# Gathered rows split on chip into three bfloat16 parts before the sums of a two-layer graph network

## The reference

```python
def sage_conv(x, src, dst, W_l, b_l, W_r, n_nodes):
    agg = segment_sum(x[src], dst)            # sum of the gathered rows of each destination
    cnt = segment_sum(ones, dst)
    return agg / maximum(cnt, 1) @ W_l.T + b_l + x @ W_r.T

h = relu(sage_conv(x, ...)); x = layernorm(x + sage_conv(h, ...))
Q, K, V = x @ Wq.T + bq, x @ Wk.T + bk, x @ Wv.T + bv;  E = edge_attr @ We.T + be
score = exp(clip((K[src] * Q[dst] / 4 * E).sum(-1), -5, 5))       # per head of 16 features
x = layernorm(x + segment_sum(V[src] * score, dst))
```

## Time and profile before

| what | us |
|---|---|
| median of three runs (13885.14 to 13908.0) | 13896.76 |
| the profiled execution, its own time | 13876.17 |
| its span, from the first to the last instruction | 13874.4 |
| POOL busy in the span | 7767.2 (56%) |
| PE busy, and its weight loads | 7655.9 (55%), 6718.6 |
| DVE busy, ACT busy | 4877.0 (35%), 2823.4 (20%) |

### The profile page before, as it was taken

How to read it: one execution, slowest core, us unless ns; L and a number is a source line. 1 busy time by engine, 2 the same in 40 slices (tenths; PEclk the granted TensorE clock), 3 DMA queues, 4 the chain that set the end, 5 groups by cost and what they waited for, 6 DMA issues and landing times.

```text
span 13874.4 us, 192542 instructions
## 1 busy us (share of the span) xinstructions
PE 7655.9 (55%) x51633; PEld 6718.6 (48%) x51634; DVE 4877.0 (35%) x11774; ACT 2823.4 (20%) x4770; POOL 7767.2 (56%) x8221
## 2 busy tenths in 40 slices
PE   5556656566666555566655555444444544444554
PEld 4555545555555445455544545444444444444444
DVE  3333333333333323233333334333333333433334
ACT  1111111111111000000000003333333333333333
POOL 5555655555555555555555555555555555555554
PEclk7666666766666666666666666555555555555555
DMA  3222222222222112111111112333333333333333
GB/s 62 50 55 52 53 50 50 49 50 49 49 49 49 42 41 46 41 42 43 41 40 41 40 40 82 101 97 98 101 95 98 98 99 90 101 92 93 99 93 82
DMA packets 951617, 917.13 MB, mean 66 GB/s; under 512 B 484896, under 2 KB 740544, under 8 KB 950544
## 3 DMA queue, kind: packets, MB, share of 16 engines
q0 software_dynamic: 260000, 369.16, 12.8%
q1 hardware_dynamic: 605345, 430.43, 11.6%
q10 hardware_dynamic: 85325, 105.63, 2.2%
HBM read 789.35 MB, written 115.24 MB: 65 GB/s over the span
## 4 chain that ended last, share of the span: by engine, by line
PE 30%; issue 30%; another core or an unknown queue 23%; DVE 7%; DVEq 7%; ACT 2%; ACTq 0%; DMA 0%; POOL 0%; POOLq 0%; SPq 0%
PE ps_kv L763 4%; PE ps_kv L754 3%; PE ps_e L740 3%; PE ps_sum L723 2%; PE ps_q L723 2%; PE ps_kv L923 2%; PE ps_hot L723 2%; PE ps_t L732 1%; ACT node_q L1037 1%; PE ps_kv L772 1%; PE ps_sum L923 1%; PE ps_hot L923 1%; PE ps_kv L903 1%; PE ps_q L923 1%
## 5 line engine op out<-in xcount | busy, mean ns | idle before, releaser
L627 POOL DMA_INDIRECT kv<-kv_rows,src_ids x3125 | 2955.6, 946 | 2344.0 <-DVE message L1520 1412.2
L627 POOL DMA_INDIRECT kv<-in_x,src_ids x2500 | 2365.3, 946 | 1845.4 <-issue 912.1
L627 POOL DMA_INDIRECT kv<-h_rows,src_ids x2500 | 2367.1, 947 | 1801.5 <-issue 955.6
L754 PE MATMUL ps_kv<-between,hot 128*128 128x490 bf16 x2500 | 897.8, 505 | 976.2 <-ACT node_q L1037 553.9
L723 PE MATMUL ps_sum<-kv,hot 128*128 128x65 f32 x5000 | 937.9, 355 | 247.7 <-issue 210.5
L723 PEld LDWEIGHTS ps_sum<-kv,hot 128*128 128x128 f32 x5000 | 922.8, 277 | 270.9 <-issue 270.2
L1086 ACT ACTIVATE node_h<-node_h,unit 128x640 bf16<-128x640 f32 x722 | 1042.6, 1444 | 36.9 <-issue 8.1
L723 PE MATMUL ps_hot<-kv 128*128 128x65 f32 x1880 | 418.9, 400 | 1075.4 <-issue 885.8
L723 PEld LDWEIGHTS ps_hot<-kv 128*128 128x128 f32 x1880 | 391.7, 309 | 1148.8 <-issue 1146.7
L754 PEld LDWEIGHTS ps_kv<-between,hot 128*128 128x128 bf16 x2500 | 291.4, 130 | 1305.9 <-issue 995.8
L1306 DVE TENSOR_SCALAR between<-ps_t,message 128x980 bf16<-128x980 f16 x1250 | 898.7, 719 | 0.0
(11 more groups left out here) (253 smaller groups left out, 12432.2 us busy)
## 6 DMA issues: line engine op xcount, KB each, us to landing
node_h<-in_dst SPq DMA_DIRECT2D x625, 320.0 KB
node_q<-in_edge_attr SPq DMA_DIRECT2D x125, 480.0 KB
edge_space<-ee_rows SPq DMA_DIRECT2D x125, 480.0 KB
kv<-kv_rows,src_ids POOLq DMA_INDIRECT x3125
kv<-in_x,src_ids POOLq DMA_INDIRECT x2500
node_q<-in_edge_attr SPq DMA_DIRECT2D x125, 320.0 KB
kv<-h_rows,src_ids POOLq DMA_INDIRECT x2500
edge_space<-ee_rows SPq DMA_DIRECT2D x125, 320.0 KB
```

The source lines that it names most:

```text
L627: nc.gpsimd.indirect_dma_start(out=into_slot, out_offset=None, in_=table_rows, in_offset=bass.IndirectOffsetOnAxis(ap=ids, axis=0),).then_ ...
L754: mm = nc.tensor.matmul(bank, place_hot[:, k, :], pair_hot[:, k, half * HALF * W:(half + 1) * HALF * W], start=(k == 0), stop=(k == K - 1))
```

## The change

In the two sums, as soon as a group has landed, its rows are split into three bfloat16 parts: ACT copies the rows to bfloat16 (high), DVE subtracts this from the rows in place (rest), ACT copies the rest to bfloat16 (middle), DVE subtracts again (low). High, middle and low lie side by side, 192 columns and a column of ones, in one of four part buffers. DVE's last step counts up `split`, and POOL now waits for this: the gathers of group n start when group n - 5 is split. The one-hots of the sums become bfloat16, and the product of a tile is one bfloat16 matmul with 193 columns (192 in the second sum). DVE adds the three parts up (`join_parts`, one reduction over two groups) before it adds to the nodes. PE does the products of a further span two groups later, behind the first product of group g + 2.

The order on the engines, at group `at`: ACT splits group `at` + 1 ahead of its copies of counts and edge products; DVE subtracts high of `at` + 1 first, and low of `at` + 1 behind the one-hots. Behind the last group of a ring nothing is split ahead: the next ring begins with the split of its group 0. Group g is split only when group g - 1 is. Buffers move for this; some constants are set at another time.

```diff
@@ POOL @@
-            gather(sum_x, sum_x.summed, 0, x, sum_rows, D)
+            gather(sum_x, sum_x.split, 0, x, sum_rows, D)
@@ PE, sum_pairs @@
-            def sum_group(to, one_hots, u, done):
+            def sum_group(to, one_hots, rows_of, width, done):
                 for k in range(K):
-                    mm = nc.tensor.matmul(to[:, 0:D + 1], one_hots[:, k, :], sum_rows[:, u, k, :],
+                    mm = nc.tensor.matmul(to[:, 0:width], one_hots[:, k, :], rows_of[:, k, 0:width],
                                           start=(k == 0), stop=(k == K - 1))
...
-                            pe.wait_ge(p.got[at % SLOTS], (T * (SUM_RING // SLOTS) + at // SLOTS) * (16 * K) + 16 * K)
-                            pe.wait_ge(p.hot, g + (1 if at % 2 else 2))
+                            pe.wait_ge(p.split, g + SLOTS + 1)
+                            if at % 2 == 0:
+                                pe.wait_ge(p.hot, g + 2)
                             hold(pe)
-                            sum_group(ps_main[at % 4], sum_hot[at % 4], at % SLOTS, p.summed)
+                            sum_group(ps_main[at % 4], sum_hot[at % 4], row_parts[at % PART_SLOTS], ROW + 1 if width > D else ROW, p.summed)
...
-                            with pe.If(more):
-                                with pe.Fori(0, more) as i:
...
-                                    sum_group(ps_further, sum_hot_x, at % SLOTS, p.x_summed)
+                            if at >= BEHIND:
+                                further(words[u], at - BEHIND)
...
+                    for i in range(BEHIND):
+                        further(words[SUM_SLOTS + i], SUM_RING - BEHIND + i)
                     sum_windows(T)
@@ ACT, edge_tiles @@
+                def split_rows(T, at):
+                    u, g = at % SLOTS, T * SUM_RING + at
+                    into = row_parts[at % PART_SLOTS]
+                    act.wait_ge(p.got[u], (T * (SUM_RING // SLOTS) + at // SLOTS) * (16 * K) + 16 * K)
+                    act.wait_ge(p.split, g + SLOTS)
+                    hold(act)
+                    nc.scalar.copy(into[:, :, 0:D], sum_rows[:, u]).then_inc(p.high, 1)
+                    act.wait_ge(p.rest, g + 1)
+                    hold(act)
+                    nc.scalar.copy(into[:, :, D:2 * D], sum_rows[:, u]).then_inc(p.middle, 1)
...
                             for u in range(SUM_SLOTS):
                                 at = j * SUM_SLOTS + u
+                                if at == 0:
+                                    split_rows(T, 0)
+                                if at + 1 < SUM_RING:
+                                    split_rows(T, at + 1)
@@ DVE @@
+            def join_parts(sums, joined):
+                return v.tensor_reduce(joined, sums[:, :, 0:ROW].rearrange("p i (s f) -> p i f s", s=SPLIT), AX, ALU.add)
...
             def add_two(p, words, at, n, nodes, count_edges):
-                add_rows(block_at(words[0][1]), ps_main[at % 4], nodes, count_edges).then_inc(p.added, 1)
+                pair = ps_pairs[at % 4 // 2]
+                join_parts(pair, added_parts).then_inc(p.joined, 1)
+                dve.wait_ge(p.joined, n)
+                add_joined(block_at(words[0][1]), added_parts[:, 0:1], pair[:, 0, ROW:ROW + 1], nodes, count_edges).then_inc(p.added, 1)
...
+            def rest_of_rows(p, T, at):
+                dve.wait_ge(p.high, T * SUM_RING + (at + 1))
+                rows_of = sum_rows[:, at % SLOTS]
+                v.tensor_tensor(rows_of, rows_of, row_parts[at % PART_SLOTS][:, :, 0:D], ALU.subtract).then_inc(p.rest, 1)
+            def low_parts(p, T, at):
+                dve.wait_ge(p.middle, T * SUM_RING + (at + 1))
+                into = row_parts[at % PART_SLOTS]
+                v.tensor_tensor(into[:, :, 2 * D:ROW], sum_rows[:, at % SLOTS], into[:, :, D:2 * D], ALU.subtract).then_inc(p.split, 1)
             def sum_ring(p, T, nodes, count_edges):
+                rest_of_rows(p, T, 0)
                 ring_numbers(p, T)
+                low_parts(p, T, 0)
...
+                        if at + 1 < SUM_RING:
+                            rest_of_rows(p, T, at + 1)
                         if at >= BEHIND:
                             dve.wait_ge(p.summed, g + (FREE + 1 - BEHIND))
...
                         sum_one_hots(g + BEHIND, block_at(words[u + 2 * BEHIND + 1][1]), sum_hot[(at + BEHIND) % 4], p.hot)
+                        if at + 1 < SUM_RING:
+                            low_parts(p, T, at + 1)
```

More of the change, by code:

```diff
@@ L273, in program @@
         assert len(ps_query) == SLOTS and QUERIES + 1 < SLOTS
-        ps_main = [bank[:, half * (D + 1):(half + 1) * (D + 1)] for bank in (ps_sum, ps_q) for half in range(2)]
+        ps_pairs = [bank[:, 0:2 * PARTED].rearrange("p (i f) -> p i f", i=2) for bank in (ps_sum, ps_q)]
+        ps_main = [pair[:, half, :] for pair in ps_pairs for half in range(2)]
         ps_extra = ps_hot32[:, 0:D]
-        ps_further = ps_hot32[:, 0:D + 1]
+        ps_further = ps_hot32[:, 0:PARTED]
+        ps_beyond = ps_hot32[:, 0:D + 1]
         ps_rows = ps_kv[0:ROWS, 0:D + 1]
@@ L352, in __init__ @@
                 if name != "att":
-                    self.x_hot, self.x_summed, self.x_added = (sem(f"{name}_x_{n}") for n in ("hot", "summed", "added"))
+                    self.high, self.middle, self.rest, self.split = (sem(f"{name}_{n}") for n in ("high", "middle", "rest", "split"))
+                    self.x_hot, self.x_summed, self.x_joined, self.x_added = (
+                        sem(f"{name}_x_{n}") for n in ("hot", "summed", "joined", "added"))
+                    self.joined = sem(f"{name}_joined")
                     self.pair_hot, self.counted, self.copied = (sem(f"{name}_{n}") for n in ("pair_hot", "counted", "copied"))
@@ L691, in split_queries @@
                 pool.wait_ge(split_done, c + 1)
-            gather(sum_x, sum_x.summed, 0, x, sum_rows, D)
+            gather(sum_x, sum_x.split, 0, x, sum_rows, D)
             pool.wait_ge(d_one.stored, 16 * CHUNKS)
-            gather(sum_h, sum_h.summed, 1, h_rows, sum_rows, D)
+            gather(sum_h, sum_h.split, 1, h_rows, sum_rows, D)
             for c in range(CHUNKS):
@@ L784, in sum_beyond, with further @@
                             hold(pe)
-                            sum_group(ps_further, sum_hot_x, SLOTS, p.o_summed)
+                            sum_group(ps_beyond, beyond_hot, beyond_rows, D + 1, p.o_summed)
+                def further(word, at):
+                    before, first, more = word
+                    with pe.If(more):
+                        with pe.Fori(0, more) as i:
+                            n = before + i
+                            pe.wait_ge(p.x_added, n + 1)
+                            pe.wait_ge(p.x_hot, n + 1)
+                            hold(pe)
+                            sum_group(ps_further, sum_hot_x, row_parts[at % PART_SLOTS], ROW + 1 if width > D else ROW, p.x_summed)
                 with pe.Fori(0, BIG) as T:
@@ L1158, in _ @@
             for p in (sum_x, sum_h):
+                for _ in range(SLOTS):
+                    v.engine_nop().then_inc(p.split, 1)
                 for _ in range(FREE):
@@ L1170, in _ @@
             v.memset(node_x1[:, :, 2 * D:], 1.0)
-            v.memset(sum_rows[:, :, :, D:D + 1], 1.0)
+            for tile in row_parts:
+                v.memset(tile[:, :, ROW:], 1.0)
+            v.memset(beyond_rows[:, :, D:], 1.0)
             v.memset(zero[:], 0.0)
```

75 lines of the change are left out of this document (45 added, 30 removed).

## The result

The kernel after takes 15,540 us (median of 4 runs, 15,501 to 15,572) against 13,891 us for the kernel before on the same chip: a ratio of 1.119, 95% interval 1.116 to 1.121. It is 11.9% slower. The forecast was 14,150 us, its range ended at 15,300.

What follows compares the result with a forecast made beforehand. It took POOL's stops in the sums, about 2060 us, as the whole stake. Stops +200 and ring ends +75 made 275 on 13876, 14,151, forecast as 14,150 us; range from 12,950 to 15,300, its own case 13,750 to 14,700.

Steps and rivals of the forecast that it cites:

- the ring's end: DVE's 25.5 us hole between rings of the sums, POOL covering it with five slots: 1.5 us a ring, +75 us.
- Products: PE's products in the sums: 0.18 us per 193-column product, net 600 us less PE time, clock 0.58 or so.
- its sign "over 0.3 us": PE's products in the sums: products of 193 columns over 0.3 us would be wrong in any case.
- The split: DVE's and ACT's added work in the sums: 1520 us more on DVE, 850 us more on ACT, neither full.
- Spans: PE's idle wait before the products of 188 further spans, 1075.4 us, 5.7 us each: this wait goes.
- What a stop then costs: POOL's stops in the sums priced like the attention's, 2.26 us a group: 2260 against 2060 us, +200 us.
- Rival B: DVE's `low_parts` behind ACT's copies and its `summed` wait sets the pace: about 15,100 us, 14,700 to 15,900; chance 0.22.
- Rival C: DVE's new subtractions, reading two SBUF tiles, hold up POOL's gathers in the sums: 980 us on top, 14,850 us; chance 0.05.
- Rival A: Credit covers POOL's stops in the sums, POOL becomes the bound: 12,850 us (half gone) to 11,820 (all); chance 0.28.

Runs made afterwards that it cites:

- the split on DVE: Kernel after with ACT's two split copies moved to DVE: 10,890 and 10,924 us, 1.041 and 1.046 to before, in batches without the hold; not run with it.

## Why the prediction was wrong

It had the direction, and missed the size by 1390 us. **The step that failed is the ring's end**, priced at +75 us; it measured +1030. The stops in the rest of the ring, priced at +200, measured +500. The remaining 112 us are longer gathers (73) and longer stretches between the sums (39), both put at nothing. Neither of the first two terms knew of the hold, without which the whole change costs 220 us.

*Products* (0.18 us each taken): 446.6/2500 = 0.18 and 205.5/1250 = 0.16. Right, by busy time over count, as the prediction had priced it. One record alone lasts 0.33 and 0.31 us, since records overlap; its sign "over 0.3 us" did not say which of the two it meant. PE is relieved by 4952 - 4037 = 915 us in the sums, not 600: the clock is 0.64 and 0.62, not 0.58, and not below 0.62 as its sign asked.

*The split.* DVE's steps take 0.49 us and its joins 0.56, as priced; ACT's copies 0.46 for 0.43. Over the whole execution ACT is 880 us busier (850 priced) and DVE 1210; of its 1520 us some 150 were waits, so 1370 were priced. Near enough.

*Spans.* "This wait goes" was wrong here: before the products of the spans PE still stands for 673.3 + 74.2 = 748 us, 4.0 us a span instead of 5.7, and the sign asked for 5. Without the hold it is 161 us.

*What a stop then costs.* Taking the attention's 2.26 us a group had the number of stops right (one in 2.5 groups; 401 of 1000), but a stop is 8.9 us, not 5.7. Without the sixth groups, which belong to the next term, it is 6.8 us and 2.4 us a group, so this price was near. That its +200 is +500 comes half from the price (2401 us against 2260) and half from what was taken off (outside the sixth groups the kernel before stood for 1904 us, not for 2060). Its premise was that the length of a stop is a property of the chain behind it. The traces show PE's signals in that chain late by 9.2 us on average where they were late by 6.2. That the length of a stop is this lateness, times the late signals that the chain needs one after another, fits the experiments but wasn't measured by itself. The prediction had noted the sign, that PE's record ends before anyone goes on and that nobody holds it ("some 5 us"; by its rows 5.9), and then carried it along as a constant. (Its own range from 13,750 to 14,700 is 13,690 to 14,690 by its terms; nothing hangs on that.)

*Ring ends.* The failed step: 1.5 us a ring, between -6.25 and +10; measured +22.6 and +20.6 before the sixth group. It assumed that DVE's hole of 25 us and POOL's 31 us of gathers run side by side. They run one after the other, since the hole begins with waits for PE, and in the timeline above these end when POOL has stopped. This term alone is 1030 us of the 1530.

*Rival B* gave 15,100 us and the case from 14,700 to 15,900, which holds the measured time, and its signs came: rings over 180 us, PE idle mostly for `split` (1313.9 and 614.0 us), DVE 2620.3 us behind ACT. The time and the place were right, the reason only in part: the chain does decide, but not by its own work and hand-overs. ACT stands in front of products whose signals are late, and where they come at once, the same order costs 2.1% in all. With the hold, the split on DVE wasn't run, so how much of the 11.9% goes through ACT's wait in particular stays open.

*Rival C* was there at a tenth of its price. 191 + 156 gathers of the sums take over 1000 ns (before 3 + 1), 342 of these 347 overlap in time with one of the new subtractions, and all together take 73 us more, 0.04 us for each of the 2000 subtractions. Without the hold it is a third of what the change costs: 71 us, against the 2365.3 and 2367.1 us above (of the kernel before without the hold only traces with pauses exist; there they are 2364.0 and 2365.3), and 156 us of stops, together 227 where 220 were measured.

*Rival A* is what happens without the hold: the stops nearly all go. But by its time they are gone in the kernel before as well (13,876 less its 2047 us of stops in the sums and 1391 in the attention is 10,440, and 10,450 was measured), so there is nothing to win.

## What to carry to other kernels

A stop in which every engine is idle and the record of the one waited for has long ended isn't slack that more buffers will fill: find what lets it go before pricing anything by it. If it is only a pause of the engine that issues or of its transfers, more credit can lengthen that engine's runs and not the cover. A deliberate short wait on it was worth 1320 us here, and cost 2000 us where nothing was held. And time a change on more than one chip: here the same two kernels stand at 1.12 or at 1.02.

## What the runs showed of the hardware

*The hold.* Shown: with it, about a third of PE's signals in the sums are late, most of them until 1 to 3.8 us after POOL's last gather, however long the products are done by the record (15.6 us in the lines above); pauses of POOL of 2.25 us a group leave 60 late of 828; kernels differ by 1.12 with it and 1.02 without; one chip had it in one batch and not in another. Not shown: what brings it about, and whether PE's results are late with its signals (the ends of products are modelled in the profile). Nor is it shown that POOL's silence is what counts. The gathered rows are a rival: in the lines above the last of them lands at 2520.1, 0.9 us before the semaphore that ACT waits for, and over the 268 signals the middle value is 2.6 us behind POOL's last gather and 1.4 us behind the last packet of its queue. No run kept POOL busy without transfers, or the reverse. Late loading of instructions is a rival that the trace speaks against: only 25 of 626 late signals of the kernel after have a packet of an instruction queue between product and signal.

*Slow sequencers.* With the hold there are stretches in which register, branch and semaphore instructions of DVE, ACT and SyncE take 0.66 to 0.74 us each: 2871 such in the kernel after, 2780 in the kernel before, mostly in the attention, and none in any run without it. PE is slow at such times too: at 1446 places of the kernel after its next weight load or product of the same line starts 0.66 to 0.74 us behind the one before (3 places without the hold), all but one while POOL gathers or within 3.8 us behind. So the lateness of PE's signals may be part of a general slowness and not a thing of PE's results. The two come and go together; which of them causes the other, or what causes both, isn't known.

*Two inputs from SBUF.* The gathers' longest time in the first sum rose little (1315 to 1318 ns), but 191 instead of 3 are over 1000. In the kernel after the 1423 gathers of both sums that overlap with a subtraction of 128 x 320 from two tiles of SBUF take 996 ns on average, 342 of them over 1000; the 3577 others take 947 ns, 5 of them over 1000. Without the hold it is 983 ns (401 over 1000) against 945 (4). So such a subtraction does lengthen a gather that it meets, by some 40 to 50 ns on average. The Trainium skill's page "SBUF — State Buffer", section "Who interferes with whom", has both halves: that two SBUF inputs contend with GpSimd's reads, and that no stall of descriptor generation was seen from such an instruction. On the second half the measurement differs: these gathers are lengthened, if only by 0.04 us a subtraction.
